# Differential attention with a ternary feed-forward part on one core: the last pair of tiles gets a pipeline of its own

## The reference

```
x = x + attn(layernorm(x))          # differential attention, 16 heads, causal
x = x + ffn(layernorm(x))

w1_q, w2_q = absmean_quant(w1), absmean_quant(w2)      # entries -1, 0, 1
h   = gelu(x @ w1_q.T + b1)         # 512 -> 2048 features, exact gelu
out = h @ w2_q.T + b2               # 2048 -> 512 features
```

## Time and profile before

| | |
|---|---|
| time, median of 3 runs (lowest, highest) | 4252.23 us (4250.93, 4252.81) |
| the profiled execution: its time, its span | 4251.76 us, 4250.0 us |
| TensorE matmul busy over the span | 3497.1 us, 82% |
| VectorE, ScalarE, GpSimd busy | 79%, 68%, 30% |
| mean granted TensorE clock | 0.947 |
| from the end of X2L of the last tile (4187.9) to the end of the span | 62.1 us |

### The profile page before, as it was taken

How to read it: one execution, slowest core, us unless ns; L and a number is a source line. 1 busy time by engine, 2 the same in 40 slices (tenths; PEclk the granted TensorE clock), 3 DMA queues, 4 the chain that set the end, 5 groups by cost and what they waited for, 6 DMA issues and landing times.

```text
span 4250.0 us, 80800 instructions
## 1 busy us (share of the span) xinstructions
PE 3497.1 (82%) x23454; PEld 2093.4 (49%) x23454; DVE 3375.8 (79%) x6194; ACT 2880.9 (68%) x6784; POOL 1259.4 (30%) x1308
## 2 busy tenths in 40 slices
PE   2688888888888888888888888888888888888886
PEld 1355555455454554545555545545545555554553
DVE  6788977889778896788877897778977789778881
ACT  1577766777667775677766777667766777667772
POOL 1232233332332313322233223332233322233323
PEclk6899999999999999999999999999999999999998
DMA  3100011000111001000011000101011000111000
GB/s 131 37 21 31 19 34 33 29 20 21 33 33 33 17 28 37 31 22 28 21 33 33 25 28 18 39 25 33 20 31 36 23 25 20 34 33 33 15 29 12
DMA packets 146816, 128.38 MB, mean 30 GB/s; under 512 B 66608, under 2 KB 117680, under 8 KB 145840
## 3 DMA queue, kind: packets, MB, share of 16 engines
q1 hardware_dynamic: 146352, 122.79, 9.0%
HBM read 67.61 MB, written 55.12 MB: 29 GB/s over the span
## 4 chain that ended last, share of the span: by engine, by line
PE 38%; DVE 24%; issue 24%; ACT 10%; POOL 2%; DVEq 1%; DMA 1%; ACTq 1%; SPq 0%; POOLq 0%
PE M L836 8%; DVE NM L683 8%; PE F L908 6%; PE SP_ L851 6%; PE M L886 5%; PE F L925 4%; PE DP L863 4%; DVE NM L691 4%; ACT E L555 2%; ACT DT L567 2%; DVE CC L703 2%; PE M L830 2%; ACT L572 2%; ACT L555 2%; DVE E L706 1%
## 5 line engine op out<-in xcount | busy, mean ns | idle before, releaser
L555 ACT ACTIVATE E<-SP_,NM 128x256 f32<-128x256 f32 (+7 forms) x2048 | 1519.7, 742 | 1011.5 <-DVE NM L691 510.2
L683 DVE TENSOR_REDUCE NM<-SP_ 128x1 f32<-128x896 f32 (+3 forms) x1024 | 1029.8, 1018 | 210.8 <-PE SP_ L852 206.2
L851 PE MATMUL SP_<-KST,QST 96*128 96x512 f16 (+3 forms) x3072 | 823.2, 339 | 418.3 <-ACT E L555 364.7
L706 DVE SCALAR_TENSOR_TENSOR E<-E,CC 128x512 f32<-128x512 f32 (+7 forms) x1024 | 928.3, 907 | 36.2
L851 PEld LDWEIGHTS SP_<-KST,QST 96*128 96x128 f16 x3072 | 269.2, 100 | 768.1 <-ACT E L555 557.3
L863 PE MATMUL DP<-ident,E 128*128 128x128 f32 x3328 | 574.0, 288 | 87.1 <-DVE E L706 76.8
L567 ACT ACTIVATE DT<-DP 128x512 f32<-128x512 f32 (+3 forms) x1024 | 523.2, 511 | 105.7 <-PE DP L863 99.4
L691 DVE TENSOR_REDUCE NM<-SP_ 128x2 f32<-128x1024 f32 (+3 forms) x512 | 419.7, 820 | 217.3 <-PE SP_ L852 197.4
L836 PE MATMUL M<-WQKV,WT 128*128 128x512 f32 x1040 | 541.2, 614 | 17.7 <-DVE TOK L747 11.0
L908 PE MATMUL F<-X2H,W1Q 128*128 128x256 f16 x2048 | 510.2, 286 | 32.2 <-DVE SQ L775 17.5
L863 PEld LDWEIGHTS DP<-ident,E 128*128 128x128 f32 x3328 | 384.8, 146 | 252.9 <-issue 132.6
(11 more groups left out here) (93 smaller groups left out, 4578.7 us busy)
## 6 DMA issues: line engine op xcount, KB each, us to landing
scratch<-SPL SPq DMA_DIRECT2D x65, 576.0 KB, 3.0
QST<-scratch SPq DMA_DIRECT2D x390, 64.0 KB, 2.3
X<-in_x SPq DMA_DIRECT2D x66, 256.0 KB, 2.7
out<-SQ SPq DMA_DIRECT2D x64, 256.0 KB, 2.0
KST<-scratch SPq DMA_DIRECT2D x390, 32.0 KB, 1.9
DT<-in_w2T SPq DMA_DIRECT2D x1, 4096.0 KB, 25.7
KST<-in_w1T SPq DMA_DIRECT2D x2, 1024.0 KB, 11.9
WQKV<-in_wqT SPq DMA_DIRECT2D x1, 1024.0 KB, 7.0
```

Of the source, the lines that this page charges most:

```text
L555: act.activation(dst, score_out(i, 2 * n + k, w), ACT.Exp, bias=NM[:, (2 * u + k) % 8:(2 * u + k) % 8 + 1], scale=1.0, accum_out=SUM[:, i ...
L683: nc.vector.tensor_reduce(NM[:, m:m + 1], score_out(i, 2 * n + k, P * (i + 1)), AX.X, ALU.max, negate=True).then_inc(max_ready, 1)
L706: nc.vector.scalar_tensor_tensor(out=E1[:, u % 4, 0:w], in0=E2[:, u % 2, 0:w], scalar=CC[:, u % 4:u % 4 + 1], in1=E1[:, u % 4, 0:w], op0=A ...
L851: pe.matmul(SP_[:, k[a // 512], 0:n], q, KST[0:ROWS, a // P:(a + n) // P, kk, :], start=True, stop=not last)
```

## The change

Pair 31 leaves the blocks: block (8, 1) has no first product any more, block (8, 2) is gone, and every engine gets a list of its own after the blocks. In it

- TensorE runs the first product piece by piece into four banks in turn (SP_[:, k % 4]), and the second product of piece k-2 after the first product of piece k. The second product has a bank for each tile, F and DP, and takes a piece for tile 0 and then for tile 1; the last piece closes both.
- ScalarE runs gelu right from the bank, with bias and scale, two instructions of 128x256 for each piece. There is no separate eviction.
- VectorE splits the even pieces and GpSimd the odd ones.
- VectorE adds b2 to x1 beforehand (two instructions) and then adds F or DP and that sum while it evicts; GpSimd's addition is gone for this pair. Tile 0 goes to OUT, tile 1 to TOK, and SyncE's queue writes both.

```diff
-        self.w1 = t % 2 == 1 and runs(3, (1,))
-        self.w2 = t % 2 == 0 and runs(4, (0, 2))
+        self.w1 = t % 2 == 1 and runs(3, ())
+        self.w2 = t % 2 == 0 and runs(4, (0,))
...
-    for t in range(3):
+    for t in range(2):
         run(QBlock(B, t, "last"))
...
+            # SyncE
+            for j in range(2):
+                sp.wait_ge(end_out, j + 1)
+                sp.dma_start(out[B - 1, (TILES - 2 + j) * P:(TILES - 1 + j) * P, :],
+                             (OUT, TOK)[j][:, :]).then_inc(o_out, 16)
...
+            # GpSimd
+            for k in range(1, FT // 2, 2):
+                h, fs = end_rows(k)
+                pool.wait_ge(end_gelu, k + 1)
+                hold(pool, f2_ready, 2 * LAST)
+                pool.tensor_scalar(HH[:, fs, :], HP[:, h, :], 1.0, 0.0, ALU.mult, ALU.add).then_inc(end_high[1], 1)
+                pool.wait_ge(end_high[1], k // 2 + 1)
+                pool.tensor_tensor(HL[:, fs, :], HP[:, h, :], HH[:, fs, :], ALU.subtract).then_inc(end_split[1], 1)
...
+            # ScalarE
+            for k in range(FT // 2):
+                h, fs = end_rows(k)
+                act.wait_ge(end_f1, k + 1)
+                if k >= 4:
+                    act.wait_ge(end_split[k % 2], (k - 4) // 2 + 1)
+                for j in range(2):
+                    ins = act.activation(HP[:, h.start + j, :], SP_[:, k % 4, 2 * P * j:2 * P * j + 2 * P], ACT.Gelu,
+                                         bias=b1c[:, fs.start + j:fs.start + j + 1], scale=1.0 / XS)
+                ins.then_inc(end_gelu, 1)
...
+            # VectorE
+            for j in range(2):
+                x1 = X1[:, (TILES - 2 + j) % 4, :]
+                nc.vector.tensor_tensor(x1, x1, b2b[:, :], ALU.add).then_inc(end_res, 1)
+            for k in range(0, FT // 2, 2):
+                h, fs = end_rows(k)
+                dve.wait_ge(end_gelu, k + 1)
+                dve.wait_ge(f2_ready, 2 * LAST)
+                nc.vector.tensor_copy(HH[:, fs, :], HP[:, h, :]).then_inc(end_high[0], 1)
+                dve.wait_ge(end_high[0], k // 2 + 1)
+                nc.vector.tensor_tensor(HL[:, fs, :], HP[:, h, :], HH[:, fs, :], ALU.subtract).then_inc(end_split[0], 1)
+            dve.wait_ge(end_res, 2)
+            dve.wait_ge(o_out, 16 * (N_TILES - 2))
+            for j in range(2):
+                dve.wait_ge(end_f2, j + 1)
+                nc.vector.tensor_tensor((OUT, TOK)[j][:, :], (F, DP)[j][:, :], X1[:, (TILES - 2 + j) % 4, :],
+                                        ALU.add).then_inc(end_out, 1)
...
+            # TensorE
+            def end_first(k):
+                if k >= 4:
+                    pe.wait_ge(end_gelu, k - 3)
+                for f in (2 * k, 2 * k + 1):
+                    for c in range(KD):
+                        for xp in (X2H, X2L):
+                            ins = pe.matmul(SP_[:, k % 4, 2 * P * (f % 2):2 * P * (f % 2) + 2 * P], W1Q[:, c, P * f:P * (f + 1)],
+                                            xp[:, c, :], start=(c == 0 and xp is X2H), stop=(c == KD - 1 and xp is X2L))
+                ins.then_inc(end_f1, 1)
+
+            def end_second(k):
+                pe.wait_ge(end_split[k % 2], k // 2 + 1)
+                for j in range(2):
+                    for f in (2 * k, 2 * k + 1):
+                        for hp in (HH, HL):
+                            ins = pe.matmul((F, DP)[j][:, :], hp[:, f, P * j:P * (j + 1)], W2Q[:, f, :],
+                                            start=(f == 0 and hp is HH), stop=(f == FT - 1 and hp is HL))
+                    if k == FT // 2 - 1:
+                        ins.then_inc(end_f2, 1)
+
+            pe.wait_ge(x2_ready, N_TILES)
+            pe.wait_ge(exp_done, B * N_E)
+            for k in range(FT // 2):
+                end_first(k)
+                if k == 2:
+                    pe.wait_ge(o_sum, 2 * LAST)
+                    pe.wait_ge(dt_ready, B * N_T)
+                if k >= 2:
+                    end_second(k - 2)
+            end_second(FT // 2 - 2)
+            end_second(FT // 2 - 1)
```

More of the change, by code:

```diff
@@ L109 @@
 N_U = H * TILES
+N_TILES = B * TILES
+LAST = N_TILES // 2 - 1
 LN1_STATS, LN1_ROWS, LN1_TURN = 1, 3, 6
@@ L138, in __init__ @@
         self.finish = runs(1, (0,))
-        self.w1 = t % 2 == 1 and runs(3, (1,))
-        self.w2 = t % 2 == 0 and runs(4, (0, 2))
+        self.w1 = t % 2 == 1 and runs(3, ())
+        self.w2 = t % 2 == 0 and runs(4, (0,))
+        self.end = kind == "last" and t == 1
         self.nb = b * TILES + t + 1
@@ L333, in diff_attention_ffn @@
         held = sem("held")
+        end_f1 = sem("end_f1")
+        end_gelu = sem("end_gelu")
+        end_high = [sem("end_high_dve"), sem("end_high_pool")]
+        end_split = [sem("end_split_dve"), sem("end_split_pool")]
+        end_res = sem("end_res")
+        end_f2 = sem("end_f2")
+        end_out = sem("end_out")
         onesf = E1[:, 0, 0:P]
@@ L361, in qk3, with end_rows @@
             return ap.rearrange("p (s d) -> p s d", d=DH)
+        def end_rows(k):
+            return slice(2 * k % GELU_F, 2 * k % GELU_F + 2), slice(2 * k, 2 * k + 2)
         block = ctx.enter_context(nc.Block())
@@ L627, in _ @@
             every_block(act, act_work)
+            act.wait_ge(h_ready, 8 * LAST)
+            for k in range(FT // 2):
[7 more added lines that the diff above has]
+                ins.then_inc(end_gelu, 1)
         @block.vector
```

## The result

The changed kernel takes 4224.1 us as the median of four runs (4222.64 to 4226.07), against 4252.52 for the kernel before in the same comparison; the ratio is 0.9933, with a 95% interval from 0.9915 to 0.9950. It is 28.4 us faster. Forecast were 4223.1 us and a gain of 29.1. The profiled execution took 4222.64 us, with a span of 4220.6.

The account below looks back on a forecast made before the run. The tail was bound by 22 us of TensorE waits and a low clock; 4188.0 + 14.0 + 13.8 + 1.65 + 0.17 + 0.73 + 2.55 = 4220.9 us span end, median 4223.1, range 4219.5 to 4229.5.

Parts of the forecast that it names:

- the sum: Last pair, from first matmul to final write: terms added up to a span end of 4220.9 us, median 4223.1.
- Start: Last pair's first matmul: waits only for X2L, no longer for bank F, so starts at 4188.00, 0.6 us earlier.
- TensorE's work: Last pair's matmuls at full clock: 14.0 us for 128 of the first product, 13.8 for 64 of the second.
- Slow start: Beginning of the last pair: TensorE at half rate for 3.3 us, losing 1.65 us; bounds 0 and 3.3.
- Waits: TensorE in the last pair: no wait for evictions or splits, 1 us as the upper bound.
- The slack of piece 7: Tightest place, the last piece's split before its second product: 0.20 us to spare, 0.0 with whole-trace means.
- Way out: After the last matmul: 0.17 us extra passage, 0.73 for VectorE, 2.55 for the write; upper bound 1 more.
- The clock rival: Last pair's matmul stream: hand-over gaps keep TensorE at 1.2 GHz, median 4248.5 us, or 4235 if half slow; chance 6%.
- The rival of the page "TensorE: Matmul & The Clock Gate": Last pair's four banks: cycling through PSUM banks makes the clock swing between two levels, with the clock rival's time.
- The hindrance rival: Splits in the last pair: VectorE and GpSimd hinder each other, a piece 1 to 2 us late, 4225 us; chance 7%.
- The slower rival: TensorE's wait for each split, uncovered: 10.1 us a piece, low clock, 4274 us, 0.5% slower; chance 2%.

Follow-up runs that it names:

- one bank and all first: Changed kernel with one first-product bank and all first product before the second: 40.5 us from X2L to the end; 4227.52 us, ratio to the kernel before 0.9946.
- gelu by halves: Changed kernel, but ScalarE evicts without gelu, then runs gelu over four pieces at once, second product four pieces behind: 41.7 us from X2L to the end.
- single file: Changed kernel with TensorE taking each piece's second product right after its first: 61.6 us from X2L to the end; 4249.66 us, ratio to the kernel before 1.0004.
- everything undone: Changed kernel with every part undone but the early start, VectorE's addition of b2 and the short last write path: 48.2 us from X2L to the end.

## Why the prediction was right

The mechanism was right: no wait of TensorE is left in the pair, and each term of the sum came out within 0.3 us. **Start.** 4188.00 forecast, 4187.99 measured. Two small errors cancel here: X2L ended 0.08 us later, and the hand-over was 0.05 instead of 0.14. **TensorE's work.** From the first start to the end of the last passage 29.6 us forecast, 29.43 measured (4187.99 to 4217.42). **Slow start.** 3.3 us at the low level and 1.65 lost were forecast. It lasted 3.0 us: fourteen steps of 0.211 us instead of 0.109 lost 1.4. That it came at all is one of two courses; the run with one bank started at full clock. **Waits.** None forecast, none found. The slack of piece 7 was put at 0.20 us and is 0.2. VectorE's instructions were priced too high, the copy at 0.7 against 0.43 to 0.58 and the subtraction at 0.8 against 0.69; gelu from the bank is 0.84 for two, as the eviction was. The two additions of b2 were priced too low, 1.6 against 2.36, because GpSimd's addition came between them (below). All this lies in slack. **Way out.** From VectorE's last end (4218.15) to the end of the span 2.45 us, 2.55 forecast. The errors, 0.0, 0.2 and 0.1, make the end 4220.6 instead of 4220.9.

**What was luck.** The sum earns the stretch, 33.0 us forecast and 32.7 measured. That the whole time came within 1.0 us of 4223.1 is in part luck. The end of X2L fell at 4187.9 in both profiled executions, though it moved by 13 us over all of them. Outside the span lay 2.04 us instead of 1.76, which hid the 0.3 of the sum in the profiled execution (4222.64, forecast 4222.7). And that execution was the fastest of the four: the median lies 1.46 above it, not 0.47.

**The clock rival** didn't come, because its condition didn't: no hand-over between pieces left a gap. Its reading of the earlier trace rows was right for those rows but too narrow. I took gaps of 1.0 us as enough for the low clock. The earlier trace rows already had a piece at full clock right after such a gap, and seven gaps in the run with one bank and all first, and others in the second execution of the kernel before, show the same. On the other hand a clock that was low stayed low through two such gaps in both executions of the kernel before. No run has such gaps in the new pipeline while its clock is low, so what they would have done there is open. The rival of the page "TensorE: Matmul & The Clock Gate" of the Trainium skill, in "A second HAM failure mode: psum-queue depth-cycling", didn't show either: with four banks in turn the clock rose once and stayed.

**The hindrance rival** cost nothing in the changed kernel. Its effect is there (below), but the splits of VectorE and GpSimd hardly meet, since the pieces come one after another: once, for 0.3 us. Where four pieces become ready at once, as with gelu by halves, they do meet, and VectorE's subtraction takes 0.98 us instead of 0.69, which lies in each of TensorE's two waits. **The slower rival** had the right place and the right waits. Its price, 10.1 us a piece and 81 in all, was too high because it let the clock stay low throughout: 61.6 were measured, at a mean clock of 0.83, and it doesn't end slower than before but equal.

**Where the gain comes from**, which the prediction had left as one difference: no part alone. From 32.7 us up, single parts undone cost about 2 (banks), 0 (alternation), 0 (shared splits), 9.0 (gelu by pieces) and 2.6 (both tiles at once); all together 15.5. Another order costs more than any of them: in single file all covers are gone, and it is 28.9. From 48.2 to the 58.5 and 62.1 us of the kernel before, 0.7 is the late start and 1.4 the longer way out (4245.01 to 4250.0 against 4217.04 to 4220.6, 5.0 against 3.6). The busy time is 4.7 to 8.3 (31.57 against 36.31 and 39.87), and that is the clock: with everything undone it was up by the second piece and stayed up, while in both executions of the kernel before it was low for three pieces at the start and for 3 us behind the wait of 5.7. Whether the low start belongs to the code, whose first matmul comes 0.7 us later there, or to chance isn't shown. So the cause of most of these 4.7 to 8.3 us stays open. The rest, 3.5, is idle time, and the waits name it, to 0.1 us: 5.7 us for GpSimd's splits, where the kernel before waits for the last four together, against 3.8 for them piece by piece; 9.2 for the evictions of the first product against 8.7; and 1.2 for the last eviction before the second product can have bank F, which the other has no need of. The late start, the way out and these three waits weren't tried alone.

## What to carry to other kernels

When one pair of tiles is alone at the end of a kernel, order its work so that something independent stands between a product and the work that needs its result. Here more banks and other work in between were interchangeable covers for the eviction, and one of them was enough. Price each part by what covers it after all the others are in, since parts undone one by one say neither what they cost together nor which is needed. Compare the tails of two profiles from a common event, not by their spans. Take a low clock seen in one profile for one possible course, until a second execution of the same kernel shows it too: here it did for the first three pieces and did not for the last three.

## What the runs showed of the hardware

**Clock.** Two courses of the same code were seen. The first matmuls of the last pair ran at 1.2 GHz for 3.0 us in the changed kernel and at 2.4 GHz from the start in the run with one bank, where the work ahead was the same. Gaps of 0.9 to 1.0 us were seen at either level. Seven of them at 2.4 GHz (one bank, all first) left the clock there; in both executions of the kernel before it stayed at 1.2 GHz from the first matmul through two of them, and was at 2.4 GHz behind the third. A wait's length alone didn't decide whether the clock was low behind it. It was low behind eight waits: 5.7 us in both executions of the kernel before, 2.7 and 2.6 with gelu by halves, three of the four of 3.0 in single file, and one of 3.0 in the first execution of the kernel before, there 1.3 us after the matmuls had begun again. It stayed at 2.4 GHz behind seven: the other of 3.0 in single file, three of 2.1 there, 2.4 in the run where one bank, all first and gelu by halves came together, and 3.0 with everything undone and in the second execution of the kernel before.

**VectorE and GpSimd at the same time.** The timeline of the changed kernel, first VectorE's two additions of b2 beside GpSimd's, then its cast beside GpSimd's split:

```profile
4188.45 2.36 DVE L859 TENSOR_TENSOR X<-X,b2b 128x512 f32<-128x512 f32 x2
4188.61 1.65 POOL L532 TENSOR_TENSOR SQ<-SQ,b2b 128x512 f32<-128x512 f32 x1 [3.46 <-DVE SQ L809]
...
4194.93 1.16 POOL L546 TENSOR_TENSOR HL<-HP,HH 128x512 f16<-128x512 f32 x1
...
4195.78 0.58 DVE L864 CAST HH<-HP 128x512 f16<-128x512 f32 x1 [2.28 <-ACT HP L659]
```

And that of the run with gelu by halves, where both split at once:

```profile
4202.66 0.43 DVE L868 CAST HH<-HP 128x512 f16<-128x512 f32 x1 [8.68 <-ACT HP L665]
...
4203.12 0.98 DVE L870 TENSOR_TENSOR HL<-HP,HH 128x512 f16<-128x512 f32 x1
...
4203.65 1.47 POOL L547 TENSOR_TENSOR HL<-HP,HH 128x512 f16<-128x512 f32 x1
...
4204.02 1.37 DVE L868 CAST HH<-HP 128x512 f16<-128x512 f32 x1
```

GpSimd's addition took 1.65 us instead of 1.26, and the two of VectorE 2.36 together, where one of that shape takes 0.69 when GpSimd rests. The second ended 0.55 us after GpSimd's, at 4190.81 against 4190.26. The cast took 0.43 us alone. Beside GpSimd's subtraction it took 0.58 when the two overlapped for 0.3 us and 1.37 when it fell almost wholly into it, and both times it ended 0.27 us after GpSimd's instruction. That is what it looks like when the second to come waits for the first to end. The Trainium skill's page "SBUF — State Buffer", section "🔬 SBUF: two separate sides", has the two exclude each other; these rows agree with it.
